# Half of a key projection between the transposes, weight parts behind the key root, and the last rows of the sparse layer first

## The chip, the core and the metric

The kernel runs on one core of one Trainium2 chip. A core has TensorE (PE, matrix products and transposes into the eight PSUM banks), VectorE (DVE), ScalarE (ACT), GpSimd (POOL) and SyncE (SP, which issues most DMAs). Each engine runs its own instructions in order and waits on semaphores for the others. The metric is the device time of one execution in microseconds; the median of three executions before the change is 1486.43 us.

## The reference, cut to what matters

The program is two transformer layers over 2048 rows of 512 (`x`), with a context of 2048 rows of 512 (`ctx`).

```python
x = x + _L0_xattn_ref(_layernorm(x), ctx, ...)   # attention with one head of 512, biases, RMS norms
x = x + _L0_ffn_ref(_layernorm(x), ...)          # sparse layer: best of 32 inner units per block
x = x + _L1_xattn_ref(_layernorm(x), ctx, ...)   # 32 heads, 8 key heads
x = x + _L1_ffn_ref(_layernorm(x), ...)          # clusters choose columns

def _L0_xattn_ref(text, features, ...):
    features_n = rmsnorm(features, fn_w)
    Q = einsum('btd,fd->btf', text, Wq_w) + Wq_b
    K = einsum('bsd,fd->bsf', features_n, Wk_w) + Wk_b
    Q = rmsnorm(Q, qn_w); K = rmsnorm(K, kn_w)
    attn = softmax(einsum('btf,bsf->bts', Q, K) * scale)
    return einsum('bts,bsf->btf', attn, features_n)
```

The change touches the first two lines and the border to the third.

## The kernel before, in words

Precision is kept by splitting each operand into a high and a low part: `split_mm` (L72 to L74) is three matmuls for one product. "Lo" work on DVE or POOL is the subtraction that makes the low part.

**First attention** (`l0_attention`). It works on 16 tiles of 128 rows. Each engine has a `body(n)`, n from 0 to 15, and all orders are written by hand. PE in `body(n)`: the key projection of tile n+1 (`project_k`, four contraction steps of three matmuls), the query projection of tile n+1 (`project_q`, twelve matmuls), the scores of tile n, the transpose of the rows of tile n+2, the attention product of tile n-1, the transposes `q_T(n+1)` (L907) and `k_T(n+1)` (L913), in tiles 11 to 14 one transpose of rows for the sparse layer (L956), and the transpose of the probabilities of tile n (L969).

The keys go round through all engines. DVE adds the key bias (L688, `s_kb`), ACT squares and sums (L532), POOL takes the root in `key_root` (L379 and L381, `s_krs`), DVE scales the keys with it (`scale_keys`, L696, `s_kn`), PE transposes them (L913). L696 reads two tensors in SBUF, the biased keys and the weights. After `k_T(n+1)` ACT copies it (L548), then the probabilities (L575), squares the queries (L540), in later tiles does a weight part (L564) and rows for the next layer (L628, L569), and then, in its next `body`, the squares of the features of a later tile (`squares_c`, L499, `s_css`). POOL starts `tile_roots(n)` (L400, L402, L406) when these are there, then makes the low part of the transposed features (`features_T`, L416), then `key_root(n+1)`, waits for `s_kn`, then the low features (`features_lo`, L411), the weighed features (`weigh`, L374), and in tiles 8 to 15 one of eight parts of the low half of the weights w1 (`split_w1`, L456, it reads two tensors in SBUF). In tile 14 alone `split_w1` stands ahead of `features_lo`, still behind the wait for `s_kn`. In tile 9 two small operations for a layernorm (L114, L116) stand behind that wait; in tiles 6 and 7 parts of other weights stand at the end (L474, L484).

**Sparse layer** (`stage_l0_attention_sparse_ffn`). Again 16 tiles. The hidden values go by halves through ACT (high part, L1251), POOL (low part, L1189) and two DMA transposes on SP (L1117, L1119) to PE, which multiplies them with w2 (`out_half`). Beside that, POOL ranks marks (L1176) for DVE, and rows of a later layernorm are split (ACT L1264, POOL L1195) and transposed by SP (L1129, L1131). For tile n = 15 these are the tiles 2 and 3 of the first chunk of the second attention. POOL does them behind the low parts of the first half; SP issues tile 2 behind the transposes of the first half and tile 3 behind those of the second half. DVE adds the product of tile 15 to x last of all (L1331, `add_out`).

**Border.** The sparse layer and the second attention are two blocks. All engines have to be through the first before any starts the second. DVE starts the second with small operations (L2554, L2555).

## Time and profile before

| | |
|---|---|
| median of three executions | 1486.43 us (1485.72 to 1488.51) |
| the profiled execution, its time | 1488.97 us |
| its span, first to last instruction | 1487.2 us |
| PE busy | 1456.9 us, 98% of the span |
| DVE, ACT, POOL busy | 1121.6, 793.4, 708.2 us |

PE is busy almost all the time; the rest of the span is its idle time. A row of a timeline gives the start and the duration of an instruction in us, the engine, the line, the operation and its tensors; in square brackets stands the idle time of the engine ahead of it and what ended that.

### The profile page before, as it was taken

The page shows a single profiled execution, that of the slowest core. Times are in us where ns is not written, and L with a number is a line of the kernel's source. Part 1 is how long each engine was busy: PE and PEld are TensorE (multiplying, and loading weights), DVE is VectorE, ACT ScalarE, POOL GpSimd, SP SyncE. Part 2 cuts the span into 40 slices and gives each one's busy share as a digit, 9 for nine tenths or more (in the row PEclk, how much of TensorE's full clock was granted, in tenths as well). Part 3 has the DMA queues.
Part 4 walks back from the last instruction along what each step waited for, and adds up shares of the span by engine and source line. Part 5 has one row for each costly group of instructions (what it writes and reads, how often), then busy time and mean ns, then how long its engine had stood idle before and what let it go on. Part 6 is the DMA issues. An engine that isn't in the chain of part 4 may idle for free.

```text
span 1487.2 us, 27765 instructions
## 1 busy us (share of the span) xinstructions
PE 1456.9 (98%) x9948; PEld 851.1 (57%) x9948; DVE 1121.6 (75%) x2161; ACT 793.4 (53%) x3201; POOL 708.2 (48%) x668
## 2 busy tenths in 40 slices
PE   8999999999999989999999999999999999999998
PEld 6888645555555555556555555655555565555554
DVE  5887787888877878676776776777677677677868
ACT  5678731211123776565556646655754664565663
POOL 6678885554665453344233434333343433343553
PEclk9999999999999999999999999999999999999999
DMA  5744445443444585534443543543454345234523
GB/s 191 239 150 141 128 90 116 106 94 82 75 82 72 118 167 90 125 86 76 110 79 66 108 99 54 102 89 78 89 93 89 82 84 106 51 66 70 103 48 114
DMA packets 359225, 148.98 MB, mean 100 GB/s; under 512 B 342336, under 2 KB 342720, under 8 KB 356144
## 3 DMA queue, kind: packets, MB, share of 16 engines
q1 hardware_dynamic: 357792, 139.87, 44.2%
q10 hardware_dynamic: 1296, 7.34, 1.5%
q8 instruction: 79, 1.29, 0.4%
q14 instruction: 58, 0.48, 0.1%
HBM read 60.11 MB, written 4.19 MB: 43 GB/s over the span
## 4 chain that ended last, share of the span: by engine, by line
PE 49%; DVE 6%; ACT 5%; POOL 3%; DMA 2%; SPq 1%; issue 1%; DVEq 0%; POOLq 0%; ACTq 0%
PE bank L72 16%; PE bank L73 15%; PE bank L74 15%; ACT a_prob L1977 3%; PE bank L2649 2%; DMA a_kT_lo<-a_kn_lo 2%; ACT a_oT_lo L1954 1%; POOL a_qrs L1849 1%; DVE a_oT_lo L2246 1%; ACT a_qr_hi L1951 1%; POOL a_prob L1831 1%; DVE a_kn L2201 1%; DVE a_qve L2185 1%; DVE x_res L2169 1%; DVE x_res L2333 1%
## 5 line engine op out<-in xcount | busy, mean ns | idle before, releaser
L1977 ACT ACTIVATE a_prob<-a_prob,a_nmx 128x64 f32<-128x64 f32 x512 | 170.2, 334 | 250.0 <-DVE a_nmx L2222 249.9
L1831 POOL TENSOR_TENSOR a_prob<-a_prob,a_mask 128x512 f32<-128x512 f32 x64 | 79.9, 1269 | 278.4 <-DVE a_prob L2216 278.4
L72 PE MATMUL bank<-w,xT_hi 128*128 128x448 f16 (+1 forms) x512 | 187.5, 366 | 1.1 <-PEq L1043 1.1
L74 PE MATMUL bank<-w,xT_hi 128*128 128x448 f16 (+1 forms) x512 | 187.3, 366 | 0.0
L73 PE MATMUL bank<-w,xT_lo 128*128 128x448 f16 (+1 forms) x512 | 187.2, 366 | 0.0
L1849 POOL TENSOR_TENSOR a_qrs<-a_qve,neg_half 128x8 f32<-128x8 f32 x64 | 104.2, 1645 | 138.9 <-DVE a_qve L2185 138.6
L1251 ACT CAST f_h_hi<-h 128x448 f16<-128x448 f32 x64 | 35.6, 563 | 207.2 <-DVE h L1325 207.1
L2169 DVE SCALAR_TENSOR_TENSOR x_res<-bank,a_oinv,x_res 128x512 f32<-128x512 f32 x128 | 95.4, 746 | 64.2 <-PE bank L74 64.2
L2174 DVE SCALAR_TENSOR_TENSOR a_qr_lo<-bank,a_qr_hi 128x512 f16<-128x512 f32 x128 | 87.9, 687 | 46.4 <-ACT a_oT_lo L1954 27.4
L1837 POOL TENSOR_TENSOR a_p_hi<-a_prob,a_rden 128x512 f16<-128x512 f32 x64 | 69.5, 1086 | 104.3 <-DVE a_rden L2230 104.3
L1189 POOL TENSOR_TENSOR f_h_lo<-h,f_h_hi 128x448 f16<-128x448 f32 x64 | 72.8, 1141 | 88.9 <-ACT f_h_hi L1251 88.9
L72 PE MATMUL bank<-w,a_cT_hi 128*128 128x256 f16 x384 | 104.7, 273 | 1.0 <-DVE a_qr_lo L2174 1.0
L73 PE MATMUL bank<-w,a_cT_lo 128*128 128x256 f16 x384 | 104.7, 273 | 0.0
L74 PE MATMUL bank<-w,a_cT_hi 128*128 128x256 f16 x384 | 104.7, 273 | 0.0
L1954 ACT ACTIVATE a_oT_lo<-bank 128x128 bf16<-128x128 f32 x400 | 103.8, 282 | 0.0
L72 PE MATMUL bank<-w,a_oT_hi 128*128 128x512 f16 x256 | 97.2, 380 | 0.8 <-DVE x_res L2169 0.8
L73 PE MATMUL bank<-w,a_xT_lo 128*128 128x512 f16 x256 | 97.5, 381 | 0.0
L72 PE MATMUL bank<-w,a_xT_hi 128*128 128x512 f16 x256 | 97.5, 381 | 0.0
L74 PE MATMUL bank<-w,a_xT_hi 128*128 128x512 f16 x256 | 97.4, 381 | 0.0
L72 PE MATMUL bank<-shared,a_oT_hi 128*128 128x512 f16 x256 | 97.2, 380 | 0.1
L1998 ACT ACTIVATE a_oT_hi<-bank 128x512 f16<-128x512 f32 x97 | 54.3, 596 | 80.1 <-PE bank L74 59.1
L73 PE MATMUL bank<-w,a_oT_lo 128*128 128x512 f16 x256 | 97.0, 379 | 0.0
(355 smaller groups left out, 4439.3 us busy)
## 6 DMA issues: line engine op xcount, KB each, us to landing
shared<-in_l_wq SPq DMA_DIRECT2D x8, 1024.0 KB, 4.9
shared<-in_l_wo SPq DMA_DIRECT2D x8, 1024.0 KB, 5.2
shared<-in_w ACTq DMA_DIRECT2D x8, 896.0 KB, 4.7
craw<-in_w SPq DMA_DIRECT2D x11, 512.0 KB, 3.8
a_wide<-in_l_ctxT SPq DMA_DIRECT2D x16, 256.0 KB, 4.0
x_res<-in_x SPq DMA_DIRECT2D x16, 256.0 KB, 4.4
shared<-in_ctx SPq DMA_DIRECT2D x16, 256.0 KB, 4.3
shared<-in_l_wkv SPq DMA_DIRECT2D x8, 512.0 KB, 4.0
```

What stands on the lines that cost most here:

```text
L72: pe.matmul(out, a_hi, b_hi, start=first, stop=False)
L73: pe.matmul(out, a_lo, b_hi, start=False, stop=False)
L74: return pe.matmul(out, a_hi, b_lo, start=False, stop=last)
L1189: pool.tensor_tensor(h_lo[:, quarter(q)], h[:, quarter(q)], h_hi[:, quarter(q)], ALU.subtract).then_inc(s_hl, 1)
L1831: pool.tensor_tensor(blocks(prob[u][:, :]), blocks(prob[u][:, :]), mask[:, :].unsqueeze(1).broadcast_to([P, NB, S]), ALU.add).then_inc(s_m ...
L1837: pool.tensor_tensor(blocks(p_hi[u][:, :]), blocks(prob[u][:, :]), share, ALU.mult).then_inc(s_ph, 1)
L1849: pool.tensor_tensor(qrs[:, half], qve[:, half], m.neg_half[:, half], ALU.pow).then_inc(s_qrs, 1)
L1954: ins = act.activation(scratch, q_banks[t][:, h * HD:(h + 1) * HD], ACT.Square, scale=SUM_DOWN, accum_out=qss[:, h % 2, t, h // 2:h // 2 + 1])
L1977: ins = act.activation(pt, pt, ACT.Exp, bias=nmx[:, col:col + 1], accum_out=den[:, col:col + 1])
L1998: ins = act.activation(oT_hi[:, u * NB:(u + 1) * NB, b * S:(b + 1) * S], blocks(pv_banks[u][b][:, :]), ACT.Copy, scale=OUT_DOWN)
L2169: dve.scalar_tensor_tensor(xt, banks[t % 2][:, :], oinv[i // NCH % 2][:, c:c + 1], xt, ALU.mult, ALU.add).then_inc(s_x, 1)
L2174: dve.scalar_tensor_tensor(qr_lo[:, t, :], q_banks[t][:, :], SUM_DOWN, qr_hi[:, t, :], ALU.mult, ALU.subtract).then_inc(s_ql, 1)
```

## The change

Four places in the first attention and the sparse layer are changed.

In PE's `body(n)` (n from 1 to 13) the first two of the four steps of the key projection of tile n+2 move between `q_T(n+1)` and `k_T(n+1)`, behind a wait for the bias of the keys of tile n+1. The next body does the other two steps.

On POOL `split_w1` moves from the end of `body(n)` to between `key_root(n+1)` and the wait for `s_kn`, for all tiles 8 to 14 (in tile 15, which has no key root, it stays where it was in effect).

In the last tile of the sparse layer POOL makes the low parts of the rows first, and SP transposes tile 2 ahead of the first half of the hidden values and tile 3 ahead of the second half.

The last `add_out` moves over the border: DVE does it in the second block in the place of a memset, PE waits for it ahead of the first `keys_values`, which writes the same bank, and DVE waits for it ahead of its statistics. The scalar `w_out` gets a place that lives longer.

```diff
@@ pool body(n) of the first attention
             if project:
                 if not first:
                     key_root(n + 1)
+            if n - 1 in SPLIT_AT:
+                split_w1(SPLIT_AT[n - 1])
+            if project:
                 pool.wait_ge(s_kn, n + 2)
             if n == ROOT_AT:
                 prep.pool_rstd(pool, 0)
-            if n == NT - 2:
-                split_w1(SPLIT_AT[n - 1])
             if project:
                 features_lo(n + 1)
             if ahead:
                 weigh(n + 2)
-            if n - 1 in SPLIT_AT and n != NT - 2:
-                split_w1(SPLIT_AT[n - 1])
@@ pe body(n) of the first attention
             if project and not first:
-                project_k(n + 1)
+                project_k(n + 1, ks=range(2, KD) if n > 1 else range(KD))
                 project_q(n + 1)
...
             elif project:
                 q_T(n + 1)
+                if ahead:
+                    pe.wait_ge(s_kb, n + 2)
+                    project_k(n + 2, ks=range(0, 2))
                 k_T(n + 1)
@@ sync, sparse layer
                 k, tiles = lo_at.get(n, (None, ()))
+                if n == NT - 1:
+                    rows_T(k, 2)
                 hidden_T(n, 0)
                 for t in tiles:
-                    if t < 3 or k == 3:
+                    if n < NT - 1 and (t < 3 or k == 3):
                         rows_T(k, t)
+                if n == NT - 1:
+                    rows_T(k, 3)
                 hidden_T(n, 1)
-                if 3 in tiles and k != 3:
+                if 3 in tiles and k != 3 and n < NT - 1:
                     rows_T(k, 3)
@@ pool, sparse layer
+                if n == NT - 1:
+                    for t in tiles:
+                        rows_lo(k, t)
                 hidden_lo(n, 0)
                 hidden_lo(n, 1)
-                k, tiles = lo_at.get(n, (None, ()))
-                for t in tiles:
-                    rows_lo(k, t)
+                if n < NT - 1:
+                    for t in tiles:
+                        rows_lo(k, t)
@@ vector, end of the sparse layer and start of the second attention
             ins.then_inc(m.wql_ok, 1)
-            add_out(NT - 1)
...
-            dve.memset(nmx[:, :], 0.0).then_inc(s_x, 1)
+            xt = m.x[:, bass.ts(NT - 1, D)]
+            dve.scalar_tensor_tensor(xt, bank[7][:, :], m.w_out[:, :], xt, ALU.mult, ALU.add).then_inc(s_x, 1)
@@ tensor, start of the second attention
             pe.wait_ge(s_cTl, 1)
+            pe.wait_ge(s_x, 1)
             keys_values(0, 0, range(TPC), 0, first_kv)
```

## Rows read from the trace of the kernel before

**Rows 1.** The page: busy time of the engines, share of the span, instructions.

```profile
PE 1456.9 (98%) x9948; PEld 851.1 (57%) x9948; DVE 1121.6 (75%) x2161; ACT 793.4 (53%) x3201; POOL 708.2 (48%) x668
```

**Rows 2.** Waits of PE over the span: for what, us in total, times, longest.

```profile
PE bank L913 <- DVE a_wide L696: 4.7, 6, 1.5
```

**Rows 3.** Tile 2 of the first attention: stretch, length, busy PE, PEld, DVE, ACT, POOL; clock.

```profile
42.70:51.70 9.00, 9.00 (x56) 7.81 (x54) 7.92 (x15) 5.86 (x15) 5.99 (x9) 1.00 0.99 225
```

**Rows 4.** Timeline of PE, the key transposes of tiles 7, 8 and 10 to 13.

```profile
97.78 0.66 PE L913 MATMUL bank<-ident,a_wide 128*128 128x128 f32 x4 [0.94 <-DVE a_wide L696]
...
107.43 0.66 PE L913 MATMUL bank<-ident,a_wide 128*128 128x128 f32 x4 [0.52 <-DVE a_wide L696]
...
126.98 0.66 PE L913 MATMUL bank<-ident,a_wide 128*128 128x128 f32 x4 [1.23 <-DVE a_wide L696]
...
136.37 0.66 PE L913 MATMUL bank<-ident,a_wide 128*128 128x128 f32 x4 [0.27 <-DVE a_wide L696]
...
145.88 0.66 PE L913 MATMUL bank<-ident,a_wide 128*128 128x128 f32 x4
...
155.40 0.66 PE L913 MATMUL bank<-ident,a_wide 128*128 128x128 f32 x4
```

**Rows 5.** Timeline of ACT, the end of the feature squares in tiles 9, 11 and 12.

```profile
110.84 0.20 ACT L499 ACTIVATION_READ_ACCUMULATOR shared<-shared 128x1 f32 x1
...
131.10 0.20 ACT L499 ACTIVATION_READ_ACCUMULATOR shared<-shared 128x1 f32 x1
...
141.04 0.19 ACT L499 ACTIVATION_READ_ACCUMULATOR shared<-shared 128x1 f32 x1
```

**Rows 6.** Timeline of POOL: tile 9's layernorm root, tile 12, tile 14's key root.

```profile
116.64 1.01 POOL L114 TENSOR_TENSOR ln_rs<-ln_ve,neg_half 128x4 f32<-128x4 f32 x1 [0.94 <-DVE a_wide L696]
...
141.36 0.20 POOL L400 TENSOR_TENSOR a_root<-a_sums,a_eps 128x3 f32<-128x3 f32 x1 [0.36 <-issue]
...
144.48 0.56 POOL L381 TENSOR_TENSOR a_krs<-a_krs,neg_half 128x1 f32<-128x1 f32 x1
145.91 1.28 POOL L411 TENSOR_TENSOR a_big<-a_wide,a_big 128x512 fp32r<-128x512 f32 x1 [0.86 <-DVE a_wide L696]
...
148.59 1.92 POOL L456 TENSOR_TENSOR w<-shared,w 128x896 f16<-128x896 f32 x1
...
162.06 0.56 POOL L381 TENSOR_TENSOR a_krs<-a_krs,neg_half 128x1 f32<-128x1 f32 x1
```

**Rows 7.** Timeline of DVE: tile 14's key scaling, and the last `add_out` of the sparse layer.

```profile
162.85 0.74 DVE L696 SCALAR_TENSOR_TENSOR a_wide<-a_wide,a_krs,shared 128x512 f32<-128x512 f32 x1
...
488.52 0.75 DVE L1331 SCALAR_TENSOR_TENSOR x_res<-bank,w_out,x_res 128x512 f32<-128x512 f32 x1 [0.41 <-PE bank L74]
```

**Rows 8.** Timeline of POOL in the second attention, two stretches.

```profile
517.81 1.04 POOL L1839 TENSOR_TENSOR a_prob<-a_prob,a_rden 128x512 f32<-128x512 f32 x1
518.81 1.15 POOL L1856 TENSOR_TENSOR a_xr_lo<-xln,a_xr_hi 128x512 f16<-128x512 f32 x1
...
575.85 3.04 POOL L1837 TENSOR_TENSOR a_p_hi<-a_prob,a_rden 128x512 f16<-128x512 f32 x1 [2.81 <-DVE a_rden L2230]
```

**Rows 9.** Timeline of DVE in the same two stretches.

```profile
518.89 1.62 DVE L2234 TENSOR_TENSOR a_p_lo<-a_prob,a_p_hi 128x512 f16<-128x512 f32 x1 [0.43 <-POOL a_prob L1839]
...
523.11 0.69 DVE L2234 TENSOR_TENSOR a_p_lo<-a_prob,a_p_hi 128x512 f16<-128x512 f32 x1 [0.47 <-POOL a_prob L1839]
...
575.69 2.30 DVE L2145 SCALAR_TENSOR_TENSOR a_cT_lo<-craw,wscale,a_cT_hi 128x2048 f16<-128x2048 f32 x1
```

**Rows 10.** Timeline of PE at the end of the sparse layer and over the border.

```profile
483.78 0.39 PE L72 MATMUL bank<-f_w_hi,f_hT_hi 128*128 128x512 f16 x1 [0.85 <-DMA f_hT_lo<-f_h_lo]
...
488.10 0.38 PE L74 MATMUL bank<-f_w_lo,f_hT_hi 128*128 128x512 f16 x1
489.60 0.38 PE L72 MATMUL bank<-w,xT_hi 128*128 128x512 f16 x1 [1.12 <-PEq L1043]
```

**Rows 11.** Waits around the start of the second attention, 487 to 540 us.

```profile
DVE a_kve L2196 <- ACT a_kn L1963: 1.9, 1, 1.9
```

More of the change, by code:

```diff
@@ L162, in persistent @@
     m.ident = sb("ident", [P, P])
-    m.ones = sb("ones", [P, 1])
+    m.ones, m.w_out = sb("ones", [P, 1]), sb("w_out", [P, 1])
     m.neg_half = sb("neg_half", [P, TPC * G])
@@ L1203, in _ @@
                 c, t = n // TPC, n % TPC
+                k, tiles = lo_at.get(n, (None, ()))
                 if n == 0:
                     split_w2(2)
+                if n == NT - 1:
+                    for t in tiles:
+                        rows_lo(k, t)
                 hidden_lo(n, 0)
                 hidden_lo(n, 1)
-                k, tiles = lo_at.get(n, (None, ()))
-                for t in tiles:
-                    rows_lo(k, t)
+                if n < NT - 1:
+                    for t in tiles:
+                        rows_lo(k, t)
                 rank_marks(n, 2)
@@ L2341, in body @@
                     dve.wait_ge(prep.shift, p0 + 3)
+                    dve.wait_ge(s_x, 1)
                     prep.dve_stats(dve, p0 + 3, 3, range(0, 1))
@@ L2820, in network @@
             fw.w1_hi, fw.w1_lo = m.w16[:, 0:KD * INTER], m.w16[:, KD * INTER:2 * KD * INTER]
-            fw.w_out = sb("w_out", [P, 1], F32)
+            fw.w_out = m.w_out
             fw.c1_raw, fw.c2_raw = sb("c1_raw", [P, KD, RK3], F32), sb("h", [P, INTER], F32)
```

## The prediction

> **What bounds the kernel now.** The page comes first: PE is busy for 98% of the span [rows 1]. So the time is PE's work plus some 30 us of idle time, and no PE work is added or removed here; the change can only move that idle time. The waits of PE come next. The largest is the key transpose L913 waiting for DVE's `scale_keys` (L696): 4.7 us in six waits; the border between the blocks costs 1.1 us [rows 10]. A quiet tile (tile 2) has PE busy for all of its 9.0 us [rows 3], so that is the least a tile can take. The timelines then show what makes `s_kn` late. Call T the end of POOL's L381, when the key root is ready. In tile 12 T is 144.48 + 0.56 = 145.04, and PE starts L913 at 145.88, T + 0.84 [rows 4, 6]. T follows the start of `tile_roots` at 141.36 by 3.68, all POOL work without a gap, and that start follows the end of ACT's feature squares at 141.23 by 0.13 [rows 5, 6]. Those squares end 4.86 after the L913 of the tile before at 136.37 [rows 4, 5]. This is a ring: L913 to ACT, to POOL, to DVE, to L913. Its length is 4.99 + 3.68 + 0.84 = 9.51, just the distance of the two L913 in tile 12 (136.37 to 145.88) [rows 4]. It is longer than it looks from PE's idle time, and each thing put into it lengthens every tile.
>
> **Weight parts behind the key root (tiles 8 to 14).** The intended gain: POOL waits 0.86 for `s_kn` ahead of L411, and L456 takes 1.92 [rows 6], so the wait would vanish under it. But L456 then starts when L381 ends, and so does L696, on the same event. What happens when a DVE instruction with two SBUF inputs meets a POOL instruction? Rows 8 and 9 show the very pattern: POOL's L1839 ends at 518.85 and releases DVE's L2234, which starts at 518.89; POOL's next, L1856, has started at 518.81. L1856 takes its 1.15, and L2234 takes 1.62 where it takes 0.69 alone: it ends 0.55 after L1856 does [rows 8, 9]. The other way round, L2145, of L696's own kind, starts 0.16 ahead of POOL's L1837, keeps its 2.30, and L1837 takes 3.04 [rows 8, 9]. So the one that starts first runs through and the other stands. In the new order L456 starts at about T - 0.04 and L696 at T + 0.04: L456 wins. L696 (0.74 alone [rows 7], so about 0.6 behind POOL's end) ends at T - 0.04 + 1.92 + 0.61 = T + 2.49 in place of T + 0.79. The key scaling is 1.7 us late, L913 starts at T + 2.54, and POOL itself waits again for `s_kn`. Bounds: if L696 won, the price is 0; if L456 were to hold it for all of its time and all of 0.75 came after, 1.8. I take 1.7, from the nearest row. The Trainium skill, page "SBUF — State Buffer", section "Who interferes with whom", says of this that a DVE instruction with two SBUF inputs contends with a GpSimd instruction that reads SBUF, and that whoever issues first makes the other block fully. By that rule a part of 1.92 us costs at most its whole length here, and the rows above agree with it.
>
> The six distances between the key transposes of tiles 7 and 13 follow. Before, they sum to 155.40 - 97.78 = 57.62 [rows 4]. New:
> Tile 7 to 8: POOL sets it (other weight parts there, no L456 ahead of T), 107.43 - 97.78 = 9.65 [rows 4], plus 1.7 at the end: 11.35.
> Tile 8 to 9: the squares end 111.04 - 107.43 = 3.61 after L913 [rows 4, 5]; 3.61 + 0.13 + 3.68 + 2.54 = 9.96.
> Tile 9 to 10: POOL sets it: L114 and its partner take about 1.25 (1.01 for the one [rows 6]), L411 to the end of `weigh` 148.59 - 145.91 = 2.68 [rows 6], then 3.68 + 2.54: 10.15.
> Tile 10 to 11: squares 131.30 - 126.98 = 4.32 after L913 [rows 4, 5]; 4.32 + 0.13 + 3.68 + 2.54 = 10.67.
> Tiles 11 to 12 and 12 to 13: 4.86 + 0.13 + 3.68 + 2.54 = 11.21 each.
> Sum 64.55, so +6.9 us. Tile 14: T is 162.62, and L696 started only at 162.85 there [rows 6, 7], so 0.2 of the 1.7 was spent already: +1.5. The scores of tile 15 and all that follows wait behind that chain. Together +8.4.
>
> **Half of the key projection between the transposes (tiles 1 to 13).** It is the same work at another place: six matmuls of 512 columns, 3072 of the 17,024 columns that PE does in a tile's 9.0 us [rows 3], 1.6 us by that share and less, since the small ones cost more for a column; I take 1.4. It fills waits of L913 up to that length, so most of the longest, 1.5 us [rows 2], which is in tile 1. But they also stand ahead of L913, so where the ring above is the bound L913 is no earlier. The added waits are free: the key root itself is made from the bias; and the low features (L416) are done before L379 and L381, some 0.8 ahead of T, so even where PE waits for them the 1.4 end at T + 0.6, before L913 could start. From tile 7 on only the head start counts by which the ring has moved: I take 0.6 us earlier at L913 of tile 7 (0 if the ring absorbs it, 1.4 if all of the filler counts). With the parts above, the first attention ends 8.4 - 0.6 = 7.8 us later. What is queued behind the late L696 on DVE (the row and key splits) keeps its distance to it. The scores have six matmuls less between `k_T` and themselves: nothing while the tiles are longer than 9.0, 1.4 once if the cover was exact. The w2 splits on POOL behind the attention hang on the last tile and shift with it.
>
> **Last rows first (tile 15 of the sparse layer).** The rows' low parts leave the place between the two halves on POOL, two instructions like L411's 1.28 [rows 6]; the rank marks and the second half come earlier by up to 2.5, and SP no longer has a row transpose between. The wait of 0.85 ahead of the last seven groups [rows 10] goes: -0.85 (0 if POOL's rows hold up a DVE select in its turn, as above).
>
> **Last add in the next block.** PE ended at 488.48, DVE's add at 489.27, PE started again at 489.60 [rows 7, 10]. Without the add the border opens 0.3 after PE: -0.8. DVE pays 0.7 more in the new block, but it stands idle for 1.9 ahead of L2196 [rows 11], on the way to the first key transposes; PE's new wait for it is behind two query products, 24 matmuls. Bounds: -0.8, and -0.1 if DVE's first operations set the pace. Taken -0.8.
>
> **Sum.** 7.8 - 0.85 - 0.8 = +6.2 us. The profiled execution took 1488.97, so 1495.2 for its like; the median of the three runs is 2.5 lower, so 1492.6. I call under 0.2% (3 us) no change, about what this measurement can tell.
>
> **Rivals.** *L696 gets through first, or shares (chance 0.11).* For: both start within 0.1 us. Against: the row at 518.89. Then the ring is as before, POOL gains its 0.86 per tile, and the distances are 9.65, three of 9.0 (PE's own work [rows 3]) and two of 9.51: 55.67, -1.95; with the head start of 0.6 and 0.3 to 0.4 at the end -3.0, and with the rest -4.65: 1481.8, faster. It decides below 0.3 us of block per tile.
> *The block is real but slack takes it (0.12).* For: POOL's own sum per tile is no longer than before, since L456 only changes places. Then tiles 8 to 11 keep their POOL-set distances and only tiles 12 to 14 pay 1 to 1.7: +2 to +3, net +1: 1487.5. Against: the feature squares follow L913 by 3.6 to 4.9 us [rows 4, 5], so POOL cannot start earlier than the late L913 lets it.
> *All seven pay in full (0.07).* 7 x 1.7 = 11.9, no head start: +10.2, 1496.7.
> The forecast has 0.70, its own range 1489.6 to 1495.5. The range over the cases is 1487.0 to 1496.0. Faster by over 0.2% (under 1483.5) 0.11, within 0.12, slower 0.77.
>
> **What would show it.** L696 at 2.4 us instead of 0.75 in tiles 8 to 14, starting 0.08 behind L456; L913 waiting 1 to 2 us in each, 10 to 11.3 us apart; POOL still waiting for L696 ahead of L411. No wait at the last `out_half`, and 0.3 us between PE's last matmul and the border. I am wrong if L696 stays at 0.75 and L456 is stretched, or if the key transposes stay 9.5 apart.

## The result and the profile after

The median after the change is 1495.95 us (1493.68 to 1498.35, six executions) against 1487.16 us (1485.33 to 1488.76, six) for the kernel before beside it: the ratio is 1.0060, with a 95% interval of 1.0047 to 1.0074, so the change costs 8.8 us (7.0 to 11.0). The forecast was 6.2 us more, 1492.6 us from a median of 1486.43. The direction and the main mechanism were right, the size 2.6 us too small.

First the page after: span, then the busy times.

```profile
span 1493.3 us, 27778 instructions
PE 1459.5 (98%) x9948; PEld 850.9 (57%) x9948; DVE 1132.2 (76%) x2160; ACT 792.2 (53%) x3201; POOL 708.5 (47%) x668
```

PE is busy for 2.6 us more than before [rows 1], though its work is the same. The waits of PE in the first attention (the kernel after, 0 to 215 us: us in total, times, longest) answer to rows 2; L695 is now `scale_keys`, L912 the key transpose. "Tile n" stands for `body(n)` here, as in the rows.

```profile
PE bank L912 <- DVE a_wide L695: 9.2, 7, 1.6
PE bank L72 <- DVE a_pT_lo L724: 1.8, 1, 1.8
PE bank L906 <- DVE a_wide L691: 1.4, 3, 0.8
```

Three waits grew: 9.2 us in seven for the scaled keys (4.7 in six before), 1.8 for the probabilities ahead of the last scores (1.4 before, below), and 1.4 for the query transpose L906, which had waited 0.2 once. Tile 8 shows the first of them, from the timelines of POOL, DVE and PE after:

```profile
106.11 0.56 POOL L381 TENSOR_TENSOR a_krs<-a_krs,neg_half 128x1 f32<-128x1 f32 x1
106.63 1.89 POOL L455 TENSOR_TENSOR w<-shared,w 128x896 f16<-128x896 f32 x1
109.15 1.28 POOL L411 TENSOR_TENSOR a_big<-a_wide,a_big 128x512 fp32r<-128x512 f32 x1 [0.63 <-DVE a_wide L695]
...
106.70 2.37 DVE L695 SCALAR_TENSOR_TENSOR a_wide<-a_wide,a_krs,shared 128x512 f32<-128x512 f32 x1 [0.77 <-POOL a_krs L381]
...
109.12 0.66 PE L912 MATMUL bank<-ident,a_wide 128*128 128x128 f32 x4 [1.61 <-DVE a_wide L695]
```

The key root ends at 106.67. POOL's weight part L455 starts at 106.63, `scale_keys` at 106.70, and it ends at 109.07, 0.55 behind the weight part. It takes 2.37 us where it took 0.74 [rows 7]. POOL has saved nothing: behind its weight part it waits 0.63 for `scale_keys` before L411. It is the pattern of rows 8 and 9. The key transposes of tiles 7 and 9 to 14, the first scores of tile 15, the second sparse tile and the start of the next block follow, in PE's timeline after:

```profile
97.87 0.66 PE L912 MATMUL bank<-ident,a_wide 128*128 128x128 f32 x4
119.19 0.66 PE L912 MATMUL bank<-ident,a_wide 128*128 128x128 f32 x4 [0.66 <-DVE a_wide L695]
129.29 0.66 PE L912 MATMUL bank<-ident,a_wide 128*128 128x128 f32 x4 [0.94 <-DVE a_wide L695]
139.87 0.66 PE L912 MATMUL bank<-ident,a_wide 128*128 128x128 f32 x4 [1.42 <-DVE a_wide L695]
150.99 0.66 PE L912 MATMUL bank<-ident,a_wide 128*128 128x128 f32 x4 [1.52 <-DVE a_wide L695]
162.12 0.66 PE L912 MATMUL bank<-ident,a_wide 128*128 128x128 f32 x4 [1.51 <-DVE a_wide L695]
171.51 0.65 PE L912 MATMUL bank<-ident,a_wide 128*128 128x128 f32 x4 [1.50 <-DVE a_wide L695]
174.76 0.44 PE L72 MATMUL bank<-a_big 128*128 128x128 f32 x1 [1.81 <-DVE a_pT_lo L724]
...
210.98 1.47 PE L1490 MATMUL bank<-f_w_lo,f_hT_hi 128*128 128x512 f16 x6 [0.32 <-POOL f_w_lo L1189]
497.90 0.38 PE L72 MATMUL bank<-w,xT_hi 128*128 128x512 f16 x1 [0.33 <-PEq L1045]
```

Before, [rows 4, 10] and these three have the same places (the key transpose of tile 14, the first scores of tile 15, the first low products of the second sparse tile):

```profile
164.51 0.60 PE L913 MATMUL bank<-ident,a_wide 128*128 128x128 f32 x4
...
167.03 0.30 PE L72 MATMUL bank<-a_big 128*128 128x128 f32 x1 [1.37 <-DVE a_pT_lo L725]
...
200.88 1.68 PE L1481 MATMUL bank<-f_w_lo,f_hT_hi 128*128 128x512 f16 x7 [0.32 <-POOL f_w_lo L1183]
```

The sum by stages, after less before, each from one execution: at the key transpose of tile 7 +0.09 (97.87 to 97.78); tiles 7 to 13 +6.63 (64.25 to 57.62); tile 14 +0.28; from there to the last scores +0.73 (3.25 to 2.52); from these to the second sparse tile +2.37 (36.22 to 33.85); to the next block -1.80 (286.92 to 288.72); from there to the end of the span -2.20 (995.4 to 997.6). Together +6.1.

The +2.37 was in no step of mine. It goes with the granted clock. Stretches of the kernel after (length, then busy us with counts of PE, PEld, DVE, ACT, POOL, then the clock, DMA share and GB/s):

```profile
core 0: us, PE busy (x) PEld busy (x) DVE busy (x) ACT busy (x) POOL busy (x), PEclk, DMA share, GB/s
170.00:172.00 2.00, 0.50 (x5) 0.49 (x5) 1.97 (x4) 0.00 (x0) 1.37 (x2) 1.00 0.07 10
172.00:174.00 2.00, 0.93 (x7) 0.50 (x5) 1.79 (x5) 1.93 (x6) 0.81 (x1) 0.85 0.82 252
174.00:176.00 2.00, 1.24 (x6) 1.27 (x7) 1.30 (x3) 2.00 (x5) 1.34 (x4) 0.50 0.00 0
180.00:182.00 2.00, 2.00 (x12) 1.24 (x10) 0.35 (x1) 0.37 (x1) 1.77 (x4) 0.95 0.35 141
```

From about 173.4 to 180.2 TensorE runs at 0.50, its level of 1.2 GHz. PE had been busy for 1.43 us of the 4 ahead of 174. That the clock makes the difference is seen across all the executions of this case: from the last scores to the second sparse tile it is 35.24 to 35.31 us where a stretch of 3.4 us at 0.50 stands there (seven executions), 36.22 to 36.91 where it is 6.8 us long (three), and 33.6 to 34.4 where there is none (nine). In the execution of the kernel before there is no such stretch here, but one in the second attention (columns as above):

```profile
536.00:540.00 4.00, 2.92 (x51) 2.29 (x52) 1.47 (x3) 1.51 (x3) 1.16 (x1) 0.75 0.39 79
540.00:544.00 4.00, 4.00 (x16) 1.63 (x15) 1.72 (x3) 3.14 (x19) 4.00 (x5) 0.83 0.86 266
```

It is 3.4 us long, so it can account for up to 1.7 of the -2.20 at the end, since after has no stretch below full clock there. That is not shown: this part varies between executions by more (see "Profile and median" below). So the sum of the two profiles, +6.1, looks just like the forecast of +6.2, and is a coincidence of one execution; the medians differ by 8.8.

### The profile page after: what moved, and what is told of

It reads as the page before. It is cut to its first block, busy times and chain, and to the rows that moved or that the text cites. A ratio compares the mean times of both kernels' runs of the same rounds, so it can differ in the third digit from the quotient of the medians.

```text
span 1493.3 us, 27778 instructions
## 1 busy us (share of the span) xinstructions
PE 1459.5 (98%) x9948; PEld 850.9 (57%) x9948; DVE 1132.2 (76%) x2160; ACT 792.2 (53%) x3201; POOL 708.5 (47%) x668
## 4 chain that ended last, share of the span: by engine, by line
PE 52%; DVE 5%; ACT 4%; POOL 2%; DMA 2%; SPq 1%; issue 1%; DVEq 0%; POOLq 0%; ACTq 0%
PE bank L72 17%; PE bank L74 16%; PE bank L73 16%; PE bank L2660 2%; ACT a_prob L1986 2%; DMA a_kT_lo<-a_kn_lo 1%; ACT a_oT_lo L1963 1%; POOL a_qrs L1858 1%; DVE a_oT_lo L2255 1%; DVE a_kn L2210 1%; ACT a_qr_hi L1960 1%; DVE x_res L2342 1%; POOL a_prob L1840 1%; DVE x_res L2178 1%; DVE a_qve L2194 0%
## 5 line engine op out<-in xcount | busy, mean ns | idle before, releaser
L1986 ACT ACTIVATE a_prob<-a_prob,a_nmx 128x64 f32<-128x64 f32 x512 | 170.2, 334 | 249.9 <-DVE a_nmx L2231 249.9
L72 PE MATMUL bank<-w,a_oT_hi 128*128 128x512 f16 x256 | 97.3, 380 | 0.3 <-DVE x_res L2178 0.3
L72 PE MATMUL bank<-w,a_xT_hi 128*128 128x512 f16 x256 | 97.1, 379 | 0.0
L74 PE MATMUL bank<-w,a_oT_hi 128*128 128x512 f16 x256 | 97.1, 379 | 0.0
L73 PE MATMUL bank<-shared,a_oT_lo 128*128 128x512 f16 x256 | 97.1, 379 | 0.0
```

The lines of the kernel that those rows point to most:

```text
L72: pe.matmul(out, a_hi, b_hi, start=first, stop=False)
L73: pe.matmul(out, a_lo, b_hi, start=False, stop=False)
L74: return pe.matmul(out, a_hi, b_lo, start=False, stop=last)
L1986: ins = act.activation(pt, pt, ACT.Exp, bias=nmx[:, col:col + 1], accum_out=den[:, col:col + 1])
```

## The experiments

All medians stand beside runs of the kernel before on the same chip (1486.1 to 1487.6 us); the ratio is what counts.

**The parts apart.** Three kernels: everything but the weight parts (the diff, against after); the weight parts alone; the last two parts alone.

```diff
-            if n - 1 in SPLIT_AT:
-                split_w1(SPLIT_AT[n - 1])
-            if project:
                 pool.wait_ge(s_kn, n + 2)
...
+            if n == NT - 2:
+                split_w1(SPLIT_AT[n - 1])
             if project:
                 features_lo(n + 1)
...
+            if n - 1 in SPLIT_AT and n != NT - 2:
+                split_w1(SPLIT_AT[n - 1])
```

> The kernel after with split_w1 put back behind the products of the features (and ahead of them in tile 14), the other three parts kept. Theory (the weight part holds scale_keys): every scale_keys (L695 of after) lasts 0.75 us again, the key transposes are 9.0 to 10.4 us apart as before, the scores of tile 15 start within 1 us of 167.0, TensorE shows no stretch below the full clock near 175, and the time is 1485 us (1483 to 1487), some 10 below after. Rival (the half key projection ahead of the key transpose, or a later part, is what costs): the key transposes stay over 10.5 us apart and the time stays above 1491.

Measured: 1.0001 (0.9992 to 1.0011), 1488.36 us. `scale_keys` takes 0.75 us in all tiles, and the extra 9 us are gone: the weight parts carry all of the loss. But 2.3 us of gain that I had for the rest are not there either. Its profiled execution has no stretch below the full clock near 175, as expected, and none in the second attention either (the only one of all), though PE waited as long ahead of the last scores as in after:

```profile
166.82 0.30 PE L72 MATMUL bank<-a_big 128*128 128x128 f32 x1 [1.81 <-DVE a_pT_lo L725]
```

> The kernel before with only split_w1 moved behind the key root. Theory (the weight part holds scale_keys): L696 lasts 2.2 to 2.4 us in tiles 8 to 14, the attention ends 7 to 8.5 us later, some 2 us more go where TensorE's clock falls to 0.5 near 175, and the time is 1497.5 us (1495 to 1500), above after by what the two later parts saved. Rival (it takes the half key projection beside it): the time is within 3 us of before.

Measured: 1.0060 (1.0047 to 1.0073), 1496.36 us, +8.9 us; the key transposes of tiles 7 to 13 take 64.24 us. The time is in the range expected. L695 takes 2.36 or 2.37 us in four tiles, and 1.87 to 1.93 in the three where it starts some 0.5 us behind the weight part and so has less of it to wait for. But the gain of the later parts, by which this kernel was to lie above after, is not there: both are at 1.0060. The last scores waited 1.81 us here too, and the clock stood at 0.5 from about 176.4 to 179.8, which is half as long as in after.

> The kernel before with the last two parts of the change alone: last rows first in tile 15 of the sparse layer, last add in the next block. My steps gave -0.85 and -0.8. Theory (both come in full and stay): no wait of PE ahead of the last out_half, the first matmul behind the border 1.65 us nearer to the first sparse tiles (489.60 less 200.88 before, 288.7; 287.0 here), the distance from there to the last matmul unchanged within 0.5 us (991.9), and the time 1485.5 to 1486.5. Rival (the second attention takes it back): the border comes 1.65 us earlier, but the waits behind it grow by as much and the time is that of before within 0.05%.

Measured: 0.9997 (0.9988 to 1.0006), 1485.29 us. The trace shows both gains: the next block starts at 486.66, 286.93 us behind the second sparse tile (288.72 before), with 0.33 us at the border:

```profile
486.66 0.38 PE L72 MATMUL bank<-w,xT_hi 128*128 128x512 f16 x1 [0.33 <-PEq L1043]
```

The time shows -0.4 us with an interval of -1.8 to +0.9. That interval contains -1.65 and it contains 0, so the gain in time is not shown.

**Who holds whom.** The rule that decides the price was tried from three sides. First a short instruction on POOL ahead of each weight part, so that `scale_keys` starts first.

```diff
             pool.wait_ge(w1h_ok, s + 1)
+            pool.memset(lead[:, :], 0.0)
             pool.tensor_tensor(fw.w1_lo[:, cols], w1_piece(s), fw.w1_hi[:, cols], ...)
```

> The kernel after with one memset of 128x1 on POOL (into a tile that nothing reads) ahead of each split_w1, so that scale_keys starts first. Theory (whoever starts first runs through, the other stands): L695 keeps 0.75 us, L455 takes 2.2 to 2.6 us instead of 1.9, POOL no longer waits for scale_keys, the key transposes are 9.0 to 9.8 us apart in tiles 8 to 14, and the time is 1484 us (1482 to 1487). Rival 1 (VectorE with two SBUF inputs stands beside any GpSimd work, whoever was first): L695 is over 2 us and the time stays at 1494 to 1497. Rival 2 (the memset does not give a lead): the same as after.

Measured: 1.0058 (1.0046 to 1.0071), 1496.87 us, no gain: rival 2. The timelines say why. The memset took 0.10 us and started before the key root had ended, so the weight part still starts 0.04 ahead of `scale_keys`:

```profile
106.75 0.10 POOL L456 MEMSET a_lead<- 128x1 f32 x1
106.80 1.89 POOL L457 TENSOR_TENSOR w<-shared,w 128x896 f16<-128x896 f32 x1
...
106.84 2.40 DVE L697 SCALAR_TENSOR_TENSOR a_wide<-a_wide,a_krs,shared 128x512 f32<-128x512 f32 x1 [0.78 <-POOL a_krs L382]
```

With two `tensor_scalar` of 128x1 in place of the memset:

```diff
+            for i in range(2):
+                pool.tensor_scalar(lead[:, i:i + 1], m.neg_half[:, 0:1], 1.0, 0.0, ALU.mult, ALU.add)
```

> As the kernel with one memset, but with two tensor_scalar of 128x1 on POOL ahead of each split_w1, each about 0.19 us by POOL's L379, so that the weight part starts some 0.2 us behind scale_keys (with the memset of 0.10 us it still started 0.04 ahead of it, at 106.80 against 106.84). Theory (whoever starts first runs through, the other stands): scale_keys keeps 0.75 us, the weight part takes 2.2 to 2.6 us, the key transposes are 9.0 to 9.8 us apart in tiles 8 to 14, and the time is 1486 us (1483 to 1489), 10 below after. Rival (VectorE with two SBUF inputs stands beside this POOL work, whoever was first): scale_keys stays over 2 us and the time is 1494 to 1498.

Measured: 0.9993 (0.9984 to 1.0001), 1485.08 us: 0.67% under the ratio of after, 10 us, with the same work at the same place and two small instructions more.

```profile
115.20 0.34 POOL L457 TENSOR_SCALAR a_lead<-neg_half 128x1 f32<-128x1 f32 x2
115.50 2.35 POOL L458 TENSOR_TENSOR w<-shared,w 128x896 f16<-128x896 f32 x1
...
115.34 0.74 DVE L698 SCALAR_TENSOR_TENSOR a_wide<-a_wide,a_krs,shared 128x512 f32<-128x512 f32 x1
```

`scale_keys` starts 0.16 ahead and keeps its 0.74; the weight part is stretched to 2.35. That is tile 9. In the other six tiles the two small instructions are themselves held beside `scale_keys` (0.85 us for both), and the weight part starts 0.01 to 0.03 us behind its end and takes its 1.9. The Trainium skill, page "SBUF — State Buffer", section "Who interferes with whom", says that whoever issues first blocks the other; these rows agree in both directions. Then the weight part was cut in two instructions of 448 columns.

```diff
-            pool.tensor_tensor(fw.w1_lo[:, cols], w1_piece(s), ...).then_inc(w1l_ok, 1)
+            for h in range(2):
+                ins = pool.tensor_tensor(fw.w1_lo[:, sub], w1_piece(s)[:, h * half:(h + 1) * half], ...)
+            ins.then_inc(w1l_ok, 1)
```

> The kernel after with split_w1 in two instructions of 448 columns each in place of one of 896. Theory A (POOL lets VectorE in where one instruction ends): scale_keys starts behind the first half, ends some 1.5 us after T, and the key transposes are 0.9 us per tile closer than in after: 1491 us (1489 to 1493). Theory B (POOL's next instruction starts before the last one has ended, 0.04 to 0.05 us in these rows, and VectorE is held through both): scale_keys takes 2.3 to 2.6 us and the time is that of after or a little more, 1496 to 1498.

Measured: 1.0032 (1.0020 to 1.0043), 1490.86 us, theory A: half of the loss is gone.

```profile
105.50 2.49 POOL L458 TENSOR_TENSOR w<-shared,w 128x448 f16<-128x448 f32 x2
...
105.57 1.52 DVE L700 SCALAR_TENSOR_TENSOR a_wide<-a_wide,a_krs,shared 128x512 f32<-128x512 f32 x1 [0.76 <-POOL a_krs L381]
```

`scale_keys` takes 1.52 us. It gets in where the first half ends (106.54), and the second half stands in its turn (2.49 for both).

**The clock.** The waits of PE in the kernel after were filled with transposes of the identity. The diff has those ahead of the key transposes, 4 to 13 of them; fourteen more stand in the last tile between `pe.wait_ge(s_kTl, n + 1)` and the scores.

```diff
+                if n >= 8:
+                    for _ in range(BUSY[n]):
+                        pe.transpose(bkT[:, 0:P], m.ident[:, :], m.ident[:, :])
                 k_T(n + 1)
```

> The kernel after with transposes of the identity into a bank that is free (0.11 us each, 4 to 14 of them) in the waits of PE ahead of the key transposes of tiles 9 to 15 and ahead of the scores of tile 15. They delay nothing. Theory (the clock falls because PE had stood idle in these waits): the key transposes start as in after, but the stretch at 0.5 from 174 to 180 is gone, the first group of low products of the sparse layer (L1490 of after, 200.96 there) starts 2.4 us earlier, and the time is 2 to 3 us below after (1493.3). Rival (the clock has another cause, or the loss is given back later): the stretch stays, or it appears elsewhere, and the time is that of after within 1 us.

Measured: 1.0063 (1.0050 to 1.0076), 1497.92 us. The stretch at half clock near 175 is gone. But the fourteen transposes did delay something, against the expectation: PE came through the wait ahead of them only at 174.00, and the scores started behind them.

```profile
174.00 1.75 PE L929 MATMUL bank<-ident 128*128 128x128 f32 x14 [1.47 <-DVE a_big L703]
175.50 0.31 PE L72 MATMUL bank<-a_big 128*128 128x128 f32 x1
```

The last scores are 4.41 us behind the last key transpose (3.25 in after), and the second sparse tile is 33.63 us behind them (36.22 in after): 2.6 us gained, 1.2 lost, so 1.4 net. (It starts at 209.13 in place of 210.98, but the key transpose of tile 14 was 0.4 earlier already, at 171.09.) And a stretch at half clock stands in the second attention now:

```profile
174.00:176.00 2.00, 2.00 (x19) 2.00 (x19) 0.89 (x2) 2.00 (x3) 1.75 (x4) 1.00 0.04 8
546.00:548.00 2.00, 2.00 (x6) 0.73 (x5) 0.89 (x3) 0.54 (x3) 1.94 (x2) 0.50 0.36 67
```

So the gain in place is shown. A gain in time is not: 1.0063 against 1.0060 in after, with intervals of 1.9 us to each side that would hide one of 1.4. Why a stretch comes in the second attention in its place is open.

**The half key projection.** I had forecast -0.6 us for it. Alone:

```diff
-                project_k(n + 1)
+                project_k(n + 1, ks=range(2, KD) if n > 1 else range(KD))
...
                 q_T(n + 1)
+                if ahead:
+                    pe.wait_ge(s_kb, n + 2)
+                    project_k(n + 2, ks=range(0, 2))
                 k_T(n + 1)
```

> The kernel before with the half key projection alone. My step gave it -0.6 us (0 to -1.4). Theory (the ring over ACT and POOL sets the key transposes from tile 7 on): PE no longer waits for scale_keys in tile 1, but L913 of tile 7 starts within 0.5 us of 97.78 and the time is that of before within 0.1%. Rival (the filler counts): L913 of tile 7 starts at 97.2 or earlier and the scores of tile 15 over 1 us earlier.

Measured: 1.0016 (1.0007 to 1.0025), 1488.54 us: +2.4 us, neither of the two. PE's timeline of it, and the clock:

```profile
41.11 0.66 PE L913 MATMUL bank<-ident,a_wide 128*128 128x128 f32 x4
76.06 0.66 PE L907 MATMUL bank<-ident,a_wide 128*128 128x128 f32 x4 [0.79 <-DVE a_wide L692]
77.93 0.60 PE L913 MATMUL bank<-ident,a_wide 128*128 128x128 f32 x4
162.56 0.66 PE L913 MATMUL bank<-ident,a_wide 128*128 128x128 f32 x4
165.82 0.30 PE L72 MATMUL bank<-a_big 128*128 128x128 f32 x1 [1.81 <-DVE a_pT_lo L725]
```

```profile
164.00:166.00 2.00, 0.19 (x3) 0.21 (x2) 1.58 (x4) 2.00 (x7) 1.92 (x4) 1.00 0.30 39
168.00:170.00 2.00, 2.00 (x7) 0.89 (x6) 0.97 (x3) 1.31 (x3) 1.83 (x2) 0.50 0.00 0
```

Two things are seen in the first of these views. L907, the query transpose, is now issued 1.4 us earlier, ahead of DVE's query bias; it waits 0.79, and the filler stands behind that wait, so that the key transpose of tile 5 comes 36.82 us behind that of tile 1 (36.31 in the kernel with the last two parts alone). And in the last tile with a key transpose, where no filler follows, PE has 1.4 us less to do. It then waits 1.81 for the probabilities in place of 1.37, and the clock is at 0.5 from about 167.5 to 170.9. Four kernels tried these two and the head start; all are the kernel before with an edit of this part alone. The first diff below adds to the kernel with the half key projection in every tile, the second and fourth stand against it, and the third shows the filler at its new place.

```diff
+            if n == NT - 1:
+                for _ in range(15):
+                    pe.transpose(bk_bank[:, 0:P], m.ident[:, :], m.ident[:, :])
             pe.wait_ge(s_kTl, n + 1)
```

> The kernel before with the half key projection alone, and 15 transposes of the identity (0.11 us each) into the free bank of the key projection while PE waits for the probabilities of tile 14 ahead of the scores of tile 15. With the half key projection alone PE stood idle there for 1.81 us, TensorE's clock was 0.5 from some 167 to 171.5, and the time was 1.0016 of before. Theory (the half key projection takes work from behind the last key transpose, the hole grows, and the clock falls after it): the scores of tile 15 start at the same place, the clock stays at 1.00 from 166 to 172, the way from L913 of tile 15 (162.56) to the first low products of the second sparse tile (201.09) is 36.3 us instead of 38.5, and the time is 1.0002 of before (0.9992 to 1.0012). Rival (its cost lies elsewhere): the time stays at 1.0016.

Measured: 1.0012 (1.0003 to 1.0021). The half clock behind the hole is gone in the profiled execution, the way from the last key transpose to the second sparse tile is 37.23 us (38.53 without the transposes, 36.3 expected), and the time is not told apart from 1.0016. The last scores stayed at 3.26 us behind the last key transpose, so here the transposes delayed nothing.

> The half key projection alone, in tiles 1 to 10 only: from tile 12 on the whole projection is behind the scores as before. Theory (the cost of this part is the hole at the end of the attention): PE's wait for the probabilities of tile 14 is 1.37 us as before and not 1.81, no stretch at half clock follows, and the time is that of before: 1.0000 (0.9990 to 1.0010). Rival 1 (the early tiles carry the cost): 1.0016. Rival 2 (my step, a head start of 0.6 us that stays): 0.9996 with the scores of tile 15 0.6 us earlier, counted from L913 of tile 1.

```diff
-                project_k(n + 1, ks=range(2, KD) if n > 1 else range(KD))
+                project_k(n + 1, ks=range(2, KD) if 1 < n < 12 else range(KD))
...
-                if ahead:
+                if n < 11:
```

Measured: 1.0010 (1.0002 to 1.0019). The wait is 1.37 again, no half clock follows, and most of the cost stays. So the hole explains a part at most.

> The kernel before with the half key projection alone, but ahead of the query transpose (L907 of before) and not between it and the key transpose. With it between them, L907 waited anew for DVE's query bias (2.4 us in five waits, 0.79 at 76.06) and the key transpose of tile 5 came at 77.93 in place of 77.46. Theory (part of its cost is its place: the query transpose, issued too early, waits, and the filler is then done behind that wait): no wait of L907 is left, L913 of tile 5 starts 36.3 us behind that of tile 1 (36.8 with the filler between, 36.3 in the kernel with the last two parts alone), and the time falls to 1.0005 of before (0.9996 to 1.0014), the hole at the end being left. Rival (the cost is all the hole at the end, or elsewhere): 1.0013 to 1.0018.

```diff
+                if ahead:
+                    pe.wait_ge(s_kb, n + 2)
+                    project_k(n + 2, ks=range(0, 2))
                 q_T(n + 1)
                 k_T(n + 1)
```

Measured: 1.0015 (1.0006 to 1.0024), the rival. The key transpose of tile 5 is 36.06 us behind that of tile 1, so the place cost what the trace showed of it, but the time is the same; the last wait is 1.81 again.

> The half key projection between the transposes in tile 1 alone, into PE's longest wait there (1.46 us); from tile 2 on the order of before. My step: work of 1.4 us leaves the way behind it, and the attention has a head start of 0.6 us (0 to 1.4) by tile 7. Theory (the ring over ACT, POOL and DVE sets the key transposes from tile 5 on): L913 of tile 3 starts up to 0.8 us nearer to that of tile 1 than 17.9, but that of tile 7 (55.6) within 0.3 us of before and the time within 0.05% of before. Rival (my step): L913 of tile 7 at 55.0 behind tile 1 or nearer and the time 0.9996 of before.

```diff
-                project_k(n + 1, ks=range(2, KD) if n > 1 else range(KD))
+                project_k(n + 1, ks=range(2, KD) if n == 2 else range(KD))
...
-                if ahead:
+                if n == 1:
```

Measured: 0.9997 (0.9988 to 1.0006), 1485.47 us, and in the trace the rival, my step, is right:

```profile
40.77 0.66 PE L913 MATMUL bank<-ident,a_wide 128*128 128x128 f32 x4
95.50 0.66 PE L913 MATMUL bank<-ident,a_wide 128*128 128x128 f32 x4 [0.94 <-DVE a_wide L696]
```

The key transpose of tile 7 is 54.73 us behind that of tile 1 (55.54 before: 97.78 [rows 4] less 42.24), and the second sparse tile 157.73 (158.64 before). Work of 1.4 us moved once into a wait gives 0.8 to 0.9 in the trace; the time (-0.4 us, -1.8 to +0.9) does not show it. Moved in every tile it gives nothing: the filler of the next tile stands in the place that is freed.

**Towards a better kernel.** Three kernels put the parts together that had gained: the last two parts and the moved weight parts, with one small instruction ahead, behind the wait (the diff), or with two ahead.

```diff
             if project:
                 pool.wait_ge(s_kn, n + 2)
+            if n - 1 in SPLIT_AT:
+                split_w1(SPLIT_AT[n - 1])
...
-            if n - 1 in SPLIT_AT and n != NT - 2:
-                split_w1(SPLIT_AT[n - 1])
```

> The kernel before with the last two parts of the change, and split_w1 behind the key root with one tensor_scalar of 128x1 on POOL ahead of it; no half key projection. Theory (scale_keys starts first and runs through, POOL works where it used to wait 0.86 us): scale_keys 0.75 us, the weight part 2.2 to 2.4 us, the key transposes of tiles 7 to 13 in 56.5 to 57.3 us (57.62 before), no hole at the end beyond 1.4 us; 1484 us, 0.998 of before (0.9970 to 0.9992). Rival (one small instruction is too short a lead): scale_keys 2.4 us and 1495.

Measured: 1.0020 (1.0011 to 1.0029), 1490.85 us. The expectation (0.998) missed by 6 us: in three of the seven tiles `scale_keys` was held. The lead decides in each tile:

```profile
105.50 0.75 DVE L697 SCALAR_TENSOR_TENSOR a_wide<-a_wide,a_krs,shared 128x512 f32<-128x512 f32 x1 [0.61 <-POOL a_krs L382]
114.48 2.45 DVE L697 SCALAR_TENSOR_TENSOR a_wide<-a_wide,a_krs,shared 128x512 f32<-128x512 f32 x1
...
105.59 2.42 POOL L457 TENSOR_TENSOR w<-shared,w 128x896 f16<-128x896 f32 x1
114.50 1.89 POOL L457 TENSOR_TENSOR w<-shared,w 128x896 f16<-128x896 f32 x1
```

With a lead of 0.09 us `scale_keys` takes 0.75; with 0.02 it is recorded first and is still held for 2.45. In tiles 10 and 14 it started behind the weight part (2.08 and 2.33).

> The kernel before with the last two parts of the change, and split_w1 for all tiles straight behind POOL's wait for scale_keys, ahead of the low products of the features. Theory (only the start beside scale_keys costs, not the place ahead of the features): scale_keys 0.75 us, POOL waits 0.86 as before, and the time is within 0.1% of before (0.9990 to 1.0005). Rival (the features' low products, 1.9 us later, become the bound of the ring or of the attended product): key transposes over 10 us apart and over 1490 us.

Measured: 0.9995 (0.9986 to 1.0004), 1485.48 us. `scale_keys` 0.75 everywhere: the place ahead of the features costs nothing, only the start beside `scale_keys` did.

> The kernel before with the last two parts of the change, and split_w1 behind the key root with two tensor_scalar of 128x1 on POOL ahead of it, as in the kernel that took this with the half key projection (0.9993 of before), but without that projection, which alone cost 1.0016. With one such instruction the lead was kept in some tiles (scale_keys at 105.50, weight part at 105.59: 0.75) and lost in others (114.48 against 114.50: 2.45). Theory: scale_keys 0.75 us in all tiles 8 to 14, the key transposes of tiles 7 to 13 in 57.0 us, and the time 0.998 of before (0.9970 to 0.9990). Rival (POOL's 0.86 us were never on the way: the ring hangs on ACT's squares in tiles 11 to 13): 0.9993 to 1.0000, as with the last two parts alone.

Measured: 1.0012 (1.0003 to 1.0021), 1488.55 us. Up to tile 14 all went as expected. In the last one `scale_keys` came late, behind DVE's own work, and had a lead of 0.04 only:

```profile
161.15 2.48 DVE L698 SCALAR_TENSOR_TENSOR a_wide<-a_wide,a_krs,shared 128x512 f32<-128x512 f32 x1
...
161.19 1.90 POOL L458 TENSOR_TENSOR w<-shared,w 128x896 f16<-128x896 f32 x1
...
166.94 0.30 PE L72 MATMUL bank<-a_big 128*128 128x128 f32 x1 [1.81 <-DVE a_pT_lo L727]
```

It was held, PE waited 1.81 ahead of the last scores, and 10.2 us at half clock in two stretches took up to 5.1 us, more than in any other kernel but the one with one instruction ahead, which has the same. Two last kernels take the filler of tile 1; the first also moves the weight parts, this tile excepted (its diff to best2), the second leaves them where they were.

```diff
-            if n - 1 in SPLIT_AT:
+            if n - 1 in SPLIT_AT and n != NT - 2:
                 split_w1(SPLIT_AT[n - 1])
...
+            if n == NT - 2:
+                split_w1(SPLIT_AT[n - 1])
```

> The kernel before with the last two parts of the change, the half key projection between the transposes in tile 1 alone, and split_w1 behind the key root with two tensor_scalar of 128x1 on POOL ahead of it, but in the last tile that has a key transpose (where scale_keys started 0.2 us late, stood 2.48 us beside the weight part and opened a wait of 1.81 us ahead of the last scores) behind the wait for scale_keys as before. Theory: scale_keys 0.75 us everywhere, the key transpose of tile 7 54.7 us behind that of tile 1, tiles 7 to 13 in 57.0 us, a wait of 1.4 us ahead of the last scores and no half clock behind it; the first low products of the second sparse tile 157.2 us behind the key transpose of tile 1 (158.64 before); 1483.5 us, 0.9980 of before (0.9970 to 0.9989). Rival (the loss of the kernels with the leading instructions is not that wait): 1.000 or above.

> The kernel before with the last two parts of the change and the half key projection between the transposes in tile 1 alone; the weight parts stay where they were. Theory (the gains seen in the traces add up): -0.85 at the key transpose of tile 7, -1.7 at the border, together 1484 us, 0.9985 of before (0.9976 to 0.9994). Rival (each is lost again in the second attention, whose length differs by 3 us from one execution to the next): 0.9995 to 1.0005.

Measured: 0.9988 (0.9979 to 0.9997), 1485.09 us, with the weight parts moved, and 0.9991 (0.9982 to 1.0000), 1485.31 us, without. Both lie in the expected ranges (0.9970 to 0.9989, 0.9976 to 0.9994), at the end with the smaller gain. The first is faster than before by 1.8 us (0.4 to 3.1), 0.7% under the kernel after; as the best of several kernels tried, it may owe part of that to chance. In its trace `scale_keys` takes 0.75 us everywhere, tiles 7 to 13 take 57.00 us (57.58 without the moved weight parts), and the second sparse tile is 157.81 us behind the key transpose of tile 1. How much of the 1.8 us is due to the weight parts is not settled: the kernel without them is within the interval. The profiled execution of that one also warns against tying the clock to the wait alone: its last wait was 1.36, and the clock still stood at 0.5 from 166.8 to 170.2.

## Where the prediction was right, and the steps that failed

**Where the 2.6 us are.** By the medians, the weight parts alone cost 8.9 us (7.0 to 10.9) against my 8.4. The other three parts together measure +0.1 (-1.2 to +1.6) where I had -0.6 - 0.85 - 0.8 = -2.25. So some 0.5 of the gap is in the weight parts, and the larger part is gain that I had counted and that the time does not show. The intervals are as wide as these terms; the traces say more of each.

**The ring and its price: right.** Forecast and measured distances of the key transposes: 11.35 and 11.25; 9.96 and 10.07; 10.15 and 10.10; 10.67 and 10.58; 11.21 and 11.12; 11.21 and 11.13; in sum 64.55 and 64.25. `scale_keys` at 2.4 us, started 0.07 behind the weight part, POOL waiting ahead of L411: each as written. The rivals are out: `scale_keys` never got through first, and no slack took it. The two small instructions ahead and the part in two halves show the cause and not only its trace, since against after they change nothing but who starts first, or for how long.

**Tile 14: too dear.** I had +1.5. In the kernel with the weight parts alone it is 9.40 us long, where it was 9.11, and the way from its key transpose to the last scores is 3.26, where it was 2.52: +1.0 together. Before, `scale_keys` of this tile ended at 163.59 [rows 7], and PE, which had other work, started L913 only at 164.51. I had not counted this slack of 0.9 us.

**The head start, -0.6: the step that failed.** I took the key transpose of tile 7 to come 0.6 us earlier. It did not: it is 55.98 us behind that of tile 1 in after and 55.54 before, and so in every kernel that has this part between the transposes in each tile up to there (55.98 to 56.13) against those without it (55.54 to 55.60). I had also called the added waits free; that the query transpose, issued earlier, would wait for DVE (0.79 us in tile 5) I had not seen. I had subtracted the work taken out of the way once, though each tile puts the same work back in; it is earned only where the filler stops. There, in the last tile, it turned into 0.44 us more of waiting. Alone this part measures +2.4 us (1.0 to 3.7). Of that, the two waits and the half clock are seen in traces; the kernels that took them away one at a time came to 1.0010 to 1.0015, so the larger part is not placed. Nor does it show in company: the last two parts measure 0.9997 without it and 1.0001 with it, intervals overlapping, and the kernels with two small instructions ahead 1.0012 without it and 0.9993 with it. That it gives no head start is shown in the traces; what it costs stays open.

**Nothing for the clock: the second step that failed.** My sum took each engine's durations as fixed. About the waits of 1.5 and 1.8 us at the end of the attention TensorE fell to its lower level for 6.8 us in the profiled execution, and the second sparse tile was 2.37 us further from the last scores. With the weight parts alone it was 3.4 us and 1.39 (35.24 to 33.85). The trace of that kernel gives the whole: 6.6 for tiles 7 to 13 (I had 6.9), 1.0 for tile 14 and the last scores (1.5), 1.4 for the clock (nothing), 9.0 in all up to the second sparse tile; the median has +8.9. That my 8.4 is near it is in part luck: one term too large stands for one left out.

**Last rows first and last add: right in place, not seen in the time.** -1.65 forecast, -1.80 in the trace of after and -1.79 in that of the two parts alone; 0.33 us at the border, no wait at the last `out_half`. The time of the two alone is -0.4 us (-1.8 to +0.9), so whether it keeps these 1.65 us is open.

**Profile and median.** I took 2.5 us off for the profiled execution of before and made the sum against it. From the next block to its end, single executions of these kernels differ by 3.6 us (from 970.50 to 974.11 between the first scores of that block and the last product of the program), the size of all the small terms together.

## What to carry to other kernels

Before a GpSimd instruction is moved into the shadow of a wait, look at what the same event releases on VectorE: if both read SBUF with two inputs, the one that starts first runs through and the other stands, and a part of 1.9 us costs 1.6 in each round of a ring that has no slack (11.12 us against 9.51 in tile 12 here). Give the critical one a lead (0.09 us was enough here, 0.04 was not), or put the other behind it. Work moved within every tile shortens nothing by itself; count it where the pattern starts and where it stops, and ask of a new hole in PE's work whether the clock stays up behind it.

## What the runs showed of the hardware

A VectorE instruction recorded 0.02 and 0.04 us ahead of GpSimd's was held for all of it (2.45 and 2.48 us); with 0.09 and more it kept 0.75. So the recorded order does not tell who goes first where the starts are 0.04 us apart or less; between 0.04 and 0.09 no row tells. A small `tensor_scalar` of 128x1 that comes behind `scale_keys` is held too: two of them take 0.34 us together ahead of it and 0.85 around it. And a stretch at half clock, 3.4 us long or 6.8, stood at the end of the first attention or near 534 to 549 in the second in 18 of 19 profiled executions, at both in four of them. A long wait goes with the first of these places but does not decide it: of the ten executions in which PE waited 1.81 or 1.82 us ahead of the last scores nine have it and one, with everything but the weight parts, has neither; of the seven that waited 1.36 or 1.37 us one has it. What it takes to keep both away no run has shown.
